# Column order of the moving operand and the output bank in five fp32r projections

## The reference, cut to what matters

```python
n  = layernorm(x)                                       # (1024, 512)
q  = n @ Wq                                             # 512 x 512, 32 heads of 16
k, v = ctx @ Wk, ctx @ Wv                               # 512 x 128 each, 8 heads of 16
q, k = rope(q, position_ids), rope(k, position_ids)
o  = softmax(q k^T / 4) v                               # within each sequence, 4 query heads per key head
x  = x + o @ Wo                                         # 512 x 512
n  = layernorm(x)
s  = (n @ Wq_w.T) @ keys.T                              # 64 expert scores per token
gate = softmax over the top 16 of s, 0 elsewhere
z  = (n @ A_w.T).reshape(-1, 64, 8) * gate[..., None]   # 512 x 512
x  = x + 2 * z.reshape(-1, 512) @ B_w.T                 # 512 x 512
```

## Time and profile before

| | |
|---|---|
| time, median of 3 runs | 168.75 us (168.11 to 169.16) |
| the profiled execution: time / span | 168.98 us / 167.3 us |
| TensorE busy | 161.8 us, 97% of the span |
| VectorE busy | 134.7 us, 81% |
| ScalarE, GpSimd busy | 95.6 us, 91.0 us |
| granted TensorE clock | 0.999 of full speed |
| mean DMA rate | 110 GB/s |

### The profile page before, as it was taken

The page is one execution under the profiler, slowest core; times in us unless marked ns, Lnnn a source line. Parts: engine busy times, 40 slices in busy tenths (PEclk is TensorE's granted clock), DMA queues, the critical chain, the costliest instruction groups (busy, mean ns, idle before and its releaser), DMA issues.

```text
span 167.3 us, 4013 instructions
## 1 busy us (share of the span) xinstructions
PE 161.8 (97%) x1341; PEld 129.7 (78%) x1341; DVE 134.7 (81%) x394; ACT 95.6 (57%) x216; POOL 91.0 (54%) x113
## 2 busy tenths in 40 slices
PE   7999999899999999999999999999999999999993
PEld 2657786777878787879797988879797866899883
DVE  1979886996998899799888989699884988667752
ACT  3588989899656453933578238732489163333210
POOL 5479999899799754725952199206340303513000
PEclk9999999999999999999999999999999999999999
DMA  4999962403315234425441344224420001000013
GB/s 157 350 414 390 407 191 66 129 13 114 105 26 162 51 89 107 106 49 182 109 109 47 104 144 101 51 55 129 106 82 0 4 0 63 8 0 0 4 63 125
DMA packets 13268, 18.45 MB, mean 110 GB/s; under 512 B 2496, under 2 KB 6208, under 8 KB 12992
## 3 DMA queue, kind: packets, MB, share of 16 engines
q1 hardware_dynamic: 12960, 17.93, 34.5%
q10 hardware_dynamic: 288, 0.27, 0.5%
HBM read 11.11 MB, written 2.10 MB: 79 GB/s over the span
## 4 chain that ended last, share of the span: by engine, by line
PE 61%; DVE 12%; SPq 10%; issue 8%; POOL 4%; ACT 3%; DMA 1%; ACTq 0%; POOLq 0%; DVEq 0%
PE ps_w L1297 8%; PE ps_w L1298 7%; PE ps_w L1302 7%; PE ps_t L1310 5%; SPq L309 5%; SPq L322 4%; DVE ps_s L984 4%; PE ps_w L1497 3%; PE ps_s L1383 3%; PE ps_t L1315 2%; PE ps_s L1417 2%; DVE o_s L1002 2%; PE ps_w L1290 2%; PE ps_w L1503 2%; PE ps_w L1292 2%
## 5 line engine op out<-in xcount | busy, mean ns | idle before, releaser
L984 DVE TENSOR_REDUCE ps_s<-ps_s 128x8 f32<-128x512 f32 x32 | 20.9, 689 | 0.6 <-PE ps_s L1383 0.3
L453 POOL TENSOR_TENSOR late<-late,gate 128x512 f32<-128x512 f32 x7 | 7.6, 1084 | 22.3 <-issue 15.8
L438 POOL TENSOR_TENSOR oT_lo<-o_n,oT_hi 128x512 fp32r<-128x512 f32 x8 | 10.4, 1296 | 15.7 <-ACT oT_hi L674 15.7
L666 ACT ACTIVATE eT<-ps_s 128x512 f32<-128x512 f32 x32 | 17.0, 602 | 2.6 <-PE ps_s L1404 1.4
L1297 PE MATMUL ps_w<-am_hi,x2T_hi 128*128 128x288 f32 x48 | 13.9, 312 | 0.0
L1298 PE MATMUL ps_w<-am_lo,x2T_hi 128*128 128x288 f32 x48 | 13.1, 294 | 0.0
L1297 PE MATMUL ps_w<-b_hi,zT_hi 128*128 128x512 f32 (+1 forms) x28 | 11.0, 399 | 0.0
L1290 PE MATMUL ps_w<-wq_hi,xT_hi 128*128 128x512 f32 x26 | 10.7, 411 | 0.0
L1298 PE MATMUL ps_w<-b_lo,zT_hi 128*128 128x512 f32 (+1 forms) x28 | 10.4, 378 | 0.0
L716 ACT ACTIVATE zT_hi<-ps_t 128x512 fp32r<-128x512 f32 x7 | 4.2, 597 | 10.8 <-PE ps_t L1310 10.8
L1292 PE MATMUL ps_w<-wq_hi,xT_lo 128*128 128x512 f32 x26 | 10.3, 394 | 0.0
(11 more groups left out here) (259 smaller groups left out, 537.9 us busy)
## 6 DMA issues: line engine op xcount, KB each, us to landing
x_sb<-x SPq DMA_DIRECT2D x8, 256.0 KB, 6.6
q_stack<-qT_hi SPq DMA_DIRECT2D x32, 64.0 KB, 2.0
cT_in<-cT SPq DMA_DIRECT2D x7, 256.0 KB, 3.0
out<-res SPq DMA_DIRECT2D x7, 256.0 KB, 2.3
wq_sb<-wq SPq DMA_DIRECT2D x4, 256.0 KB, 5.4
late<-wo SPq DMA_DIRECT2D x1, 1024.0 KB, 7.7
am_sb<-aT SPq DMA_DIRECT2D x1, 1024.0 KB, 8.8
b_sb<-bT SPq DMA_DIRECT2D x1, 1024.0 KB, 7.2
```

The lines of the kernel that those rows point to most:

```text
L438: pool.tensor_tensor(oT_lo[:], o_n[:].rearrange("p (b r q) -> p r b q", b=2, r=REP), oT_hi[:].bitcast(F32), ALU.subtract).then_inc(oT_lo_o ...
L666: act.activation(eT[:, c].rearrange("p b n -> p (b n)"), ps_s[:, c, :], ACT.Exp)\
L984: dve.tensor_reduce(neg_top[:, b, HALF_H * half:HALF_H * (half + 1), :], ps_s[:, 2 * (1 - b) + half, :].rearrange("p (r h k) -> p h r k", ...
```

## The change

Only the three helpers change. A table keyed by the weight's high part gives an order, and the same order is laid over the output bank and the moving operand of every product of that projection, so that each column of the weights still adds into the column of the bank that it had. `woven(run)` cuts the columns into two halves and takes `run` columns from the first, `run` from the second, and so on: 4 columns for `wq`, 16 for `wo`, 2 for `am`, 32 for `wkv`. `backward` takes the columns of `b` from the last to the first. Stationary operands, the number of products, their sequence, the waits and all other engines' lists stay.

```diff
@@ -1285,21 +1285,34 @@
 
         @block.tensor
         def _(pe):
+            def woven(run):
+                def order(a):
+                    return a.rearrange("p (i j e) -> p j i e", i=2, e=run)
+                return order
+
+            def backward(a):
+                return a[:, ::-1]
+
+            ORDER = {"wq_hi": woven(4), "wo_hi": woven(16), "b_hi": backward, "am_hi": woven(2), "wkv_hi": woven(32)}
+
             def product(dst, hi, lo, w_hi, w_lo, cols, chunks=range(DK)):
+                order = ORDER[w_hi.name]
                 for k in chunks:
-                    pe.matmul(dst, hi(k), w_hi[:, k, cols], start=(k == 0), stop=False)
-                    pe.matmul(dst, hi(k), w_lo[:, k, cols], start=False, stop=False)
-                    mm = pe.matmul(dst, lo(k), w_hi[:, k, cols], start=False, stop=(k == DK - 1))
+                    pe.matmul(order(dst), hi(k), order(w_hi[:, k, cols]), start=(k == 0), stop=False)
+                    pe.matmul(order(dst), hi(k), order(w_lo[:, k, cols]), start=False, stop=False)
+                    mm = pe.matmul(order(dst), lo(k), order(w_hi[:, k, cols]), start=False, stop=(k == DK - 1))
                 return mm
 
             def high_part(dst, hi, w_hi, w_lo, cols, chunks=range(DK)):
+                order = ORDER[w_hi.name]
                 for k in chunks:
-                    pe.matmul(dst, hi(k), w_hi[:, k, cols], start=(k == 0), stop=False)
-                    pe.matmul(dst, hi(k), w_lo[:, k, cols], start=False, stop=False)
+                    pe.matmul(order(dst), hi(k), order(w_hi[:, k, cols]), start=(k == 0), stop=False)
+                    pe.matmul(order(dst), hi(k), order(w_lo[:, k, cols]), start=False, stop=False)
 
             def low_part(dst, lo, w_hi, cols, chunks=range(DK)):
+                order = ORDER[w_hi.name]
                 for k in chunks:
-                    mm = pe.matmul(dst, lo(k), w_hi[:, k, cols], start=False, stop=(k == DK - 1))
+                    mm = pe.matmul(order(dst), lo(k), order(w_hi[:, k, cols]), start=False, stop=(k == DK - 1))
                 return mm
 
             def chunk(t):
```

## The result

The changed kernel takes 179.68 us (179.48 to 180.32, 4 runs) against 168.95 us (168.11 to 169.32, 4 runs): ratio 1.0645, 95% interval 1.0608 to 1.0681. It is slower by 6 to 7%, outside the range of the forecast. Its profiled execution takes 179.48 us with a span of 177.8 us, 10.5 us more than before.

What follows compares the result with a forecast made beforehand. TensorE was taken to bound the kernel, its column time coming out nearly whole. Moving operand's order, output bank's order and extra pattern level were each 0, sum 0, so 168.8 us; range 167.0 to 175.0 us.

Steps and rivals of the forecast that it cites:

- What bounds the kernel: TensorE, busy 161.8 of 167.3 us and 61% of the chain; added column time comes out nearly whole.
- The price of products and their count: Five projections: 552 products at 232.5, 132.5 or 117.5 ns for 512, 288 or 256 columns, together 98.1 us.
- The moving operand's order ... I take 0: TensorE's read of the weights' columns in another order costs 0, bounded between -6.9 and +98.1 us.
- small cost of 1 to 4%: TensorE's changed products pay a small cost per jump or product: 170.5 to 175 us, chance 0.08.
- rival 2: Each jump between runs in TensorE's products costs a 0.449 ns step: 18.9 us more, 187.7 us, chance 0.05 in full.
- The output bank's order ... I take 0: TensorE's writes to the output bank in another order cost 0, with the same bounds as the moving operand's.
- The extra level of the pattern: One more pattern level in 444 woven products: 0 taken, +1.1 us if it doubled the fixed 2.5 ns a product.
- Rival 1: Reversal costs, weaving doesn't: b's products take a step for each column, 22.4 us more, 190 us, chance 0.09.
- Rivals 3 and 5: 3: all out-of-order columns take two steps, +98.1 us, chance 0.03; 5: build restores rising order, 168.8 us, within forecast's 0.70.
- Rival 4: Alternating halves or the reverse removes the projections' column time above the clock: 6.9 us at most, about 162 us, chance 0.05.
- The weighed rule: Skill on TensorE's orders: PSUM page says non-contiguous patterns slow matmuls, unpriced; errata wants consecutive elements together, read as 0.

Runs made afterwards that it cites:

- run 15: Kernel before with split weights stored as even and odd column halves, TensorE reading one column from each in turn: 168.80 us against 168.54, ratio 1.0006.
- run 9: Kernel before with all five projections out of order on both sides, every four columns kept in their 16 bytes: 169.35 us against 169.28, ratio 0.9993.
- 11: Kernel before with wq pairs turned, wo fours turned, am steps of 3, wkv halves alternating (moving operand alone), b pairs from 64 streams (both sides): 211.91 us.

## Why the prediction was wrong

- **What bounds the kernel:** right. The page, the waits and the chain said that TensorE's time comes out nearly whole, and 11.9 us in the projections came out as 10.5. In the other direction the prediction named VectorE at 81% as what might eat a gain. TensorE did stand for VectorE's rotated keys (2.47 us in run 15), but VectorE was itself waiting, through ScalarE, for a token tile.
- **The price of products and their count:** right; the kernel before stood at 132.9, 117.7 and 233 ns throughout.
- **"The moving operand's order ... I take 0":** this is the step that failed. Its size is 11.9 us, inside the bounds that stood there (-6.9 to +98.1), but the value was taken from rows that couldn't carry it: VectorE reading blocks of 8 columns of a bank, and a weight load with a step of zero, which stays on one column. Neither takes a part of an aligned 16 bytes of SBUF and goes on to another stretch, and am does. Between a small cost of 1 to 4% (chance 0.08) and rival 2 in full (11%, 0.05) the prediction left a gap, and the measured 6.4% fell into it.
- **"The output bank's order ... I take 0":** right, and shown with the bank alone (169.52 us in one execution, all spacings as before but b's halves, which came out some 4 ns shorter).
- **The extra level of the pattern:** 0 for am in run 9. The other woven weights there moved by +2 (wq), +4 (wo) and -2 ns (wkv); whether the level has a part in that is not shown. It stays within the 1.1 us allowed for.
- **Rival 1, the reverse costs:** wrong. b keeps 235 ns (runs 9 and 11 agree: turned fours 233 ns).
- **Rival 2, each jump costs 0.449 ns:** for am it named 65 ns and 55 came (187.9 less 132.9), for wkv 4 and some 3; for wq it named 57 and some 20 came, for wo 14 and some 7. Near am it looks right and is not: the same 144 jumps inside 16 bytes cost nothing.
- **Rivals 3 and 5:** no spacing doubled in the change, and since the times moved, the orders did reach the engine.
- **Rival 4, a faster order exists:** it had no place in this change, but the limit is real: 0.42 ns a column with two streams of single columns, and it gave nothing measurable at the end; what the traces show of its loss are waits and a fallen clock that the prediction hadn't named.
- **The weighed rule:** of the Trainium skill's two statements, the PSUM page's general one found no support on the bank; "Advanced Engine Details and Errata", Memory Cachelines, points to the right place, the 16-byte stretch of SBUF, but two hits on it were not enough here: two of four columns cost 1.3 to 1.8 ns a visit, four of four 1.8.

What is shown: the loss is in the read, four fifths of it (9.8 of 11.9 us) at am's runs of 2, and it vanishes when the runs stay in their 16 bytes. What stays open is why. Counting stretches gives the numbers of runs of 2 off and on the grid, but not the equal price of steps of 2 and 4 (0.9 ns a column), nor 0.42 ns for single columns from two halves, nor the small cost of distant aligned runs (wq's fours 20 ns, wo's sixteens 7 ns a product), where near fours cost at most 2.

## What to carry to other kernels

Walk an fp32r moving operand so that each four columns in succession are one aligned 16-byte stretch. Their order inside it, the order of stretches close by, and the tried orders on the output bank were free here, while runs of 2 from distant places, steps, and single columns from eight or more places cost 1.4 to 2.2 times the column time. Where no row shows the access that an edit introduces, the nearest row must be near in the property that changes (here, how many bytes lie together), and not only in engine or operation. And read gains and losses apart: an engine at 97% passes a loss on almost whole, but a gain only down to the next wait.

## What the hardware showed that was not expected

| fp32r moving operand, spacing less 2.5 ns over columns | ns a column |
|---|---|
| one column from each of two halves in turn | 0.42 |
| rising; reversed; pairs or fours exchanged nearby | 0.45 |
| sixteens, thirty-twos exchanged nearby | 0.46, 0.44 |
| rising from 4 or 8 bytes off the 16-byte grid; runs of 16 or 32 from two halves | 0.46 to 0.47 |
| runs of 4 or 8 from two halves | 0.47 to 0.49 |
| one column, or a run of 4, from each of four quarters | 0.52 to 0.54 |
| runs of 2 from two halves, or runs of 4 off the 16-byte grid | 0.64 to 0.66 |
| runs of 2 from three parts | 0.73 |
| runs of 2 from 4 to 128 parts; steps of 2, 3, 4; one column from each of 8 or 32 parts | 0.85 to 0.98 |

Rising order, then, is not the fastest: at a granted clock of 1.0 it runs 7% below one column a cycle of 2.4 GHz, and two alternating streams of single columns close that gap (512 columns in 216 ns against 233).
